# A two-layer graph kernel: the last item of layer two in four short sides and two batches, a later load of the path words, and saves by block

## The reference

```python
h = relu(layernorm(x))
# layer one: graph convolution with W, b; norm from the degrees
x = x + relu(segment_sum(norm[:, None] * (h @ W.T + b)[row], col))
h = relu(layernorm(x))
# layer two: rows of 16 segments x 32; 64 paths (i1, i2, i3) with coefficients
x1 = h[src].reshape(-1, 16, 32)
x2 = edge_attr_512.reshape(-1, 16, 32)
contrib = path_coeffs[None, :, None] * x1[:, i1, :] * x2[:, i2, :]
edge_out = zeros.at[:, i3, :].add(contrib)
out = zeros.at[dst].add(edge_out)          # x + out is returned
```

## Time and profile before

| | us |
|---|---|
| median of 3 runs (lowest, highest) | 1154.01 (1152.04, 1155.46) |
| the profiled execution's own time | 1154.45 |
| its span in the trace | 1152.8 |
| PE busy | 841.4 (73%) |
| DVE busy | 890.8 (77%) |
| ACT busy | 420.1 (36%) |
| POOL busy | 533.6 (46%) |
| mean granted TensorE clock | 0.849 of full speed |

### The profile page before, as it was taken

One profiled execution on the slowest core, in us unless ns is written; L12 is line 12 of the kernel. 1 busy time (PEld: TensorE's weight loads), 2 busy tenths in 40 slices (PEclk: granted clock), 3 DMA queues, 4 the chain that ended last, 5 costly groups with the idle time before them and its releaser, 6 DMA issues.

```text
span 1152.8 us, 21994 instructions
## 1 busy us (share of the span) xinstructions
PE 841.4 (73%) x5118; PEld 405.0 (35%) x5119; DVE 890.8 (77%) x1955; ACT 420.1 (36%) x1612; POOL 533.6 (46%) x610
## 2 busy tenths in 40 slices
PE   2788779990686967778696777859587785951985
PEld 1344333440341514324151432416142341510465
DVE  4667768440798989989898998989899898964600
ACT  4887886336024042332405133240513324013040
POOL 3222210435746555664656566465556656123010
PEclk9799998995887988989798898979988898985965
DMA  8000002135856556775655577575656767324000
GB/s 154 1 0 0 0 1 74 37 119 173 297 211 235 185 193 217 260 260 212 241 185 194 208 260 260 212 252 186 221 182 246 260 230 252 102 107 106 1 11 7
DMA packets 58553, 183.07 MB, mean 159 GB/s; under 512 B 19940, under 2 KB 20068, under 8 KB 52588
## 3 DMA queue, kind: packets, MB, share of 16 engines
q0 software_dynamic: 28528, 88.43, 24.4%
q1 hardware_dynamic: 21048, 88.36, 20.4%
q10 hardware_dynamic: 8900, 5.55, 1.8%
HBM read 173.45 MB, written 8.86 MB: 158 GB/s over the span
## 4 chain that ended last, share of the span: by engine, by line
DVE 31%; DVEq 25%; PE 20%; issue 15%; POOL 3%; ACT 2%; DMA 2%; SPq 1%; POOLq 0%; ACTq 0%
DVE q_mem L735 28%; DVEq L291 11%; DVEq L729 9%; PE psum L1067 5%; PE psum L1053 4%; PE psum L974 3%; PE psum L985 3%; PE psum L1008 2%; DVEq L735 2%; POOL x_mem L522 2%; DVE x_mem L656 1%; PE psum L999 1%; PE psum L971 1%; DMA x_mem<-in_L_gnn_W 1%; ACT hot_mem L823 1%
## 5 line engine op out<-in xcount | busy, mean ns | idle before, releaser
L735 DVE TENSOR_TENSOR q_mem<-x_mem 128x448 f32 (+1 forms) x1334 | 722.7, 622 | 104.6 <-DMA x_mem<-h_rows,src_now 55.6
L1067 PE MATMUL psum<-q_mem,hot_mem 128*32 128x512 f32 x2584 | 419.4, 719 | 206.5 <-DVE q_mem L735 193.9
L522 POOL DMA_INDIRECT x_mem<-h_rows,src_now x323 | 399.6, 1237 | 269.2 <-DVE q_mem L735 175.4
L1067 PEld LDWEIGHTS psum<-q_mem,hot_mem 128*32 128x32 f32 x2584 | 100.2, 127 | 485.5 <-issue 376.0
L1053 PEld LDWEIGHTS psum<-S,ident 128*128 128x128 f32 x1664 | 203.1, 203 | 33.3 <-issue 33.3
L1053 PE MATMUL psum<-S,ident 128*128 128x32 f32 x1664 | 208.6, 287 | 0.0
L908 ACT ACTIVATE S<-psum,coef 128x32 f32<-128x32 f32 (+1 forms) x832 | 153.1, 369 | 128.1 <-PE psum L1067 105.5
L914 ACT ACTIVATE acc<-psum 128x512 f32<-128x512 f32 x13 | 7.8, 597 | 456.7 <-PE psum L1053 391.3
L656 DVE TENSOR_SCALAR x_mem<-x_mem,spare 128x320 bf16<-128x320 f16 x324 | 79.1, 301 | 39.8 <-issue 39.8
L518 POOL DMA_DIRECT2D out<-acc x55 | 49.3, 896 | 105.7 <-ACT acc L914 82.6
L985 PE MATMUL psum<-x_mem,hot_mem 128*128 128x320 bf16 x324 | 68.4, 338 | 28.7 <-DVE x_mem L656 14.1
(11 more groups left out here) (156 smaller groups left out, 399.2 us busy)
## 6 DMA issues: line engine op xcount, KB each, us to landing
x_mem<-in_edge_attr SPq DMA_DIRECT2D x44, 1024.0 KB
x_mem<-in_edge_attr SPq DMA_DIRECT2D x44, 768.0 KB
x_mem<-h_rows,src_now POOLq DMA_INDIRECT x323
x_mem<-in_edge_attr SPq DMA_DIRECT2D x2, 1792.0 KB
out<-acc POOLq DMA_DIRECT2D x55, 64.0 KB
x_mem<-in_x SPq DMA_DIRECT2D x1, 2304.0 KB
out<-x_mem ACTq DMA_DIRECT2D x9, 256.0 KB
h_rows<-x_mem ACTq DMA_DIRECT2D x9, 256.0 KB, 2.0
```

Source lines behind the costliest of these rows:

```text
L522: pool.indirect_dma_start(x1[:, t, :], None, h2_dram[:, :], bass.IndirectOffsetOnAxis(ap=now[:, t - first:t - first + 1].bitcast(u32), axis=0)
L735: return nc.vector.tensor_tensor(q[s % 2][:, 0:tiles, p % PG, :], x1[:, first:first + tiles, ds(a, U)], x2[:, first:first + tiles, ds(b, U ...
L1067: last = nc.tensor.matmul(ps[g][side * M:(side + 1) * M, :], hot[:, first + k, :], q[s % 2][:, k, :, :].rearrange("p n u -> p (n u)"), sta ...
```

## The change

Five things, beside the renaming that follows from them.

1. **Last item.** FULL now counts full items (11). The 1826 edges of the last are four sides of 4, 4, 4 and 3 tiles (2 whole and one of 34 edges), cut in two batches of 8 and 7 tiles (`CUT_LAST`). POOL, DVE, ACT and PE run their ordinary two-batch code on it, SP a `load_last` with a wait for each batch. The final `save` takes each block after its own slot of the second batch. The last adds are four sides instead of three. COLS is 323. Indices are loaded by four DMAs for `dst` and four for `src` instead of two each; DVE's preparation has a few small reduces, copies and subtractions more.
2. **First turn.** The edge rows of three sides instead of two are loaded while layer one runs (`EARLY`), and the fourth waits for `agg_summed` alone. To make room, `counts_b`, `iota_i` and the pieces in `parts` are put elsewhere.
3. **Saves.** `save` gets the slots it waits for as a list. In the turns it is `[0, 1, G - 1, G - 1]`: blocks 2 and 3 both wait for slot 7 of the turn before, where block 2 waited for slot 6. In the final `save` it is each block's own slot.
4. **Blocks** are taken from `ORDER` and `ORDER_END`, both `[0, 1, 2, 3]`, which is the order of before.
5. **Path words.** DVE loads the next six words after the fourth product of six (`p % CHUNK == CHUNK // 2`), where it did after the first. This isn't in the change's title.

```diff
-    TL = 2 * T + 1
-    NORMAL, LAST_ITEM = [T, T, T, T], [T, T, 1, 1]
+    TL = 4
+    REST = E - FULL * P * TI
+    TR, TAIL = divmod(REST - (S4 - 1) * P * TL, P)
+    NORMAL, LAST_ITEM = [T] * S4, [TL] * (S4 - 1) + [TR + 1]
     CUT = [[(0, 4), (0, 4), (0, 3), (0, 3)], [(4, 7), (4, 7), (3, 7), (3, 7)]]
-    CUT_LAST = [(0, T), (0, T), (0, 1)]
+    CUT_LAST = [[(0, TL // 2)] * S4, [(TL // 2, n) for n in LAST_ITEM]]
+    ORDER, ORDER_END = [0, 1, 2, 3], [0, 1, 2, 3]
+    EARLY = 3
...
-            sp.dma_start(dst_i[:, 0:FULL * T].rearrange("p (b t) -> p b t", t=T), dst_full).then_inc(idx_in, 16)
-            sp.dma_start(dst_i[0:TAIL, FULL * T:FULL * T + 1], dst_tail).then_inc(idx_in, 16)
+            for to, edges in zip(by_column(dst_i), by_partition(dst)):
+                sp.dma_start(to, edges).then_inc(idx_in, 16)
...
                     for s in range(S4):
-                        if j == 0 and s == 2:
+                        if j == 0 and s == EARLY:
                             sp.wait_ge(agg_summed, C)
-                            for i in range(2):
-                                sp.wait_ge(h2_stored[i], 16 * (C // 2))
...
-            def load_last(turn):
-                sp.wait_ge(multiplied, group_before(turn, G - 1))
-                for s in range(2):
-                    if s:
-                        sp.wait_ge(multiplied, group_before(turn, TURN - 1))
-                    sp.dma_start(x2_mem[:, s * T * D:(s + 1) * T * D], edge_full[:, FULL - 2 + s, :]).then_inc(x2_last, 16)
-                sp.dma_start(x2[0:TAIL, 2 * T, :], edge_tail).then_inc(x2_last, 16)
+            def load_last(window, turn):
+                for j in range(2):
+                    at = tiles_before(CUT_LAST[j])
+                    sp.wait_ge(multiplied, group_before(turn, j * G + G - 1))
+                    if j:
+                        n = tiles_before(CUT_LAST[0])[-1]
+                        sp.wait_ge(x1_last[0], window * (16 * n) + 16 * n)
+                    for s in range(S4):
...
-            def gather_last(window, turn, at):
-                now = src_now[:, 0:TL]
-                for j in range(2):
-                    pool.wait_ge(multiplied, group_before(turn, j * G + G - 1))
...
-            for s in range(S4 - 1):
+            for s in range(S4):
                 add_rows(s, newer, total + 1)
...
                 for p in range(block * PG, min((block + 1) * PG, SURE)):
                     last = product(s, first, tiles, p)
-                    if p < STEADY and p % CHUNK == 0:
+                    if p < STEADY and p % CHUNK == CHUNK // 2:
                         load_pairs(p // CHUNK + 1)
-                last.then_inc(multiplied, done)
+                last.then_inc(multiplied, 1)
...
             def product_last(window, turn, at):
-                dve.wait_ge(x1_last, window * (16 * TL) + 16 * TL)
-                dve.wait_ge(x2_last, window * 48 + 48)
-                for g in range(G):
-                    product_slot(turn, g, 0, TL, 1 if g < G - 1 else 1 + G)
+                for j in range(2):
+                    n = tiles_before(CUT_LAST[j])[-1]
+                    dve.wait_ge(x1_last[j], window * (16 * n) + 16 * n)
+                    dve.wait_ge(x2_last[j], window * (16 * S4) + 16 * S4)
+                    for g, block in enumerate(ORDER if j == 0 else ORDER_END):
+                        product_slot(turn, j * G + g, block, j * TB, n)
...
-            def save(turn):
+            def save(turn, slots_done):
                 act.wait_ge(mixed, turn + 1)
-                for g in range(G):
-                    act.wait_ge(summed, group_before(turn, G + g))
-                    for p in range(g * PG, (g + 1) * PG):
+                for block in range(G):
+                    act.wait_ge(summed, group_before(turn, G + slots_done[block]))
+                    for p in range(block * PG, (block + 1) * PG):
...
                     if j == 0:
-                        save(turn)
+                        save(turn, [0, 1, G - 1, G - 1])
...
-            save(total)
+            save(total, ORDER_END)
```

More of the change, by code:

```diff
@@ L121, in gnn_layers_kernel @@
         in_agg, in_hot = Carve(x2_mem), Carve(hot_mem)
-        in_agg.take(2 * 4 * D)
+        in_agg.take(sum(b - a for a, b in CUT[0][0:EARLY]) * D)
         counts_b = in_agg.take(C * CW // 2).bitcast(bf16).rearrange("p (c n) -> p c n", c=C)
@@ L206, in gnn_layers_kernel @@
         acc = sb("acc", [P, D], fp32)
-        in_sums = Carve(S)
-        homes = ([in_hot.take(D // 2) for i in range(TI * M // (D // 2))]
-                 + [in_sums.take(D // 2) for i in range(NP * U // (D // 2))]
-                 + [in_iota.take(D // 2) for i in range(CW // (D // 2))])
-        homes += [in_agg.take(D // 2) for i in range(PARTS * C - len(homes))]
-        assert in_agg.at <= TI * D
+        more = sb("more", [P, 3 * (D // 2)], fp32)[:, :]
+        in_idx.at = 0
+        homes = []
+        for carve in (in_hot, Carve(S[:, :]), in_q, in_idx, Carve(bias_b), Carve(more), in_agg):
+            while carve.at + D // 2 <= carve.mem.shape[1] and len(homes) < PARTS * C:
+                homes.append(carve.take(D // 2))
+        assert len(homes) == PARTS * C
         parts = [[homes[i * C + c].bitcast(bf16) for c in range(C)] for i in range(PARTS)]
@@ L743, in late_products, with product_slot @@
                             product(s, first, tiles, m)
[L745 to L746 removed]
+            def product_slot(turn, s, block, first, tiles):
                 dve.wait_ge(summed, group(turn, s - 2))
                 dve.sem_inc(vector_steps, 1)
[L749 removed]
+                if block == G - 1:
                     late_products(s, first, tiles, SURE)
[L751 removed]
+                for p in range(block * PG, min((block + 1) * PG, SURE)):
                     last = product(s, first, tiles, p)
[L753 removed]
+                    if p < STEADY and p % CHUNK == CHUNK // 2:
                         load_pairs(p // CHUNK + 1)
[L755 removed]
+                last.then_inc(multiplied, 1)
             load_pairs(0)
@@ L1056, in mix, with sum_slot @@
                     last.then_inc(mixed, 1)
-            def sum_slot(turn, s, cut, first, begin, end, done):
-                g, at = s % G, tiles_before(cut)
+            def sum_slot(turn, s, block, cut):
+                j, at = s // G, tiles_before(cut)
                 pe.wait_ge(multiplied, group(turn, s))
@@ L1066, in sum_slot, with sum_turn @@
                             k = at[side] + t
-                            last = nc.tensor.matmul(ps[g][side * M:(side + 1) * M, :], hot[:, first + k, :],
+                            last = nc.tensor.matmul(ps[block][side * M:(side + 1) * M, :], hot[:, j * TB + k, :],
                                                     q[s % 2][:, k, :, :].rearrange("p n u -> p (n u)"),
-                                                    start=(begin and t == 0), stop=(end and t == b - a - 1))
-                last.then_inc(summed, done)
-            def sum_turn(window, turn, at):
+                                                    start=(j == 0 and t == 0), stop=(j == 1 and t == b - a - 1))
+                last.then_inc(summed, 1)
+            def sum_turn(turn, cuts, orders):
                 for j in range(2):
                     pe.wait_ge(hot_ready, turn * 2 + (j + 1))
-                    for g in range(G):
-                        sum_slot(turn, j * G + g, CUT[j], j * TB, j == 0, j == 1, 1)
+                    for g, block in enumerate(orders[j]):
+                        sum_slot(turn, j * G + g, block, cuts[j])
                         if j == 0:
```

182 lines of the change are left out of this document (88 added, 94 removed).

## The result

The changed kernel takes **1181.28 us** (median of 4 runs, 1174.66 to 1204.30), against 1153.83 (1152.04 to 1155.46, 4 runs) before: slower, by a ratio of 1.022 (95% interval 1.015 to 1.029; it leaves out the longest run, which stands over 1.5% above the shortest, and with all four the medians give 1.024). I had forecast 1128. The four times spread over 30 us, where those of before spread over 3. The profiled execution is the longest of the four (1204.30, span 1202.6); what it shows is one arrangement of a delay that comes and goes, so I use its rows for what happens, and the runs' times for how much.

A forecast was written before the change was run, and what follows sets the result against it. DVE's products were taken to bound the turns, PE close behind. Last product's end 1085.0, plus tail 48.0, minus steady 8, plus 1.5 gave a span of 1126.5; with 1.65 outside the span, 1128 us, range 1112 to 1144.

The forecast's parts named there:

- Start of each batch: DVE's batches in the turns: loading words behind the fourth product saves 0.88 us per first batch, 0.36 to 0.45 per second.
- The slower rival: Late saves throttle PE in every turn and its clock falls: 4.4 us in each of 10 turns, about 1180 us; chance 0.06.
- the sign: PE's granted clock in the turns changing by more than 0.03 from 0.849 would show the forecast wrong.
- Steady sum: All turns together: second batches -4.6 us, first batches -3.5 after PE and late saves, in sum -8; bounds -15 to +2.
- the later load buys nothing: Rival for the turns: lead is lost at long loads or PE sets slot 4; steady 0, 1136 us; chance 0.16.
- Last item: DVE's last-item products: hole gone, sequencer bounds batches of 24.9 and 30.3 us, last product ends at 1085.0 against 1089.8: -5.
- the rival of the lower clock in the last item: Item 10's four mixes on PE cost 6.9 us each instead of 3.76: 1138 us; chance 0.09.
- Tail: From the last product to the span's end: 48.0 us instead of 63.0, so -15, with final mixes of 27.3.
- The rival of full clock: Final mixes on PE run at full speed, 15.0 us instead of 27.3: 1116 us; chance 0.12.
- The rest: Preparation before layer two: more index DMAs and small DVE operations cost +1.5 us, bounds 0 and +3; other small terms about 0.

The follow-up runs named there:

- e1: Changed kernel with the six words loaded behind the first product of six again: 1135.21 us, ratio 0.984 to the kernel before.
- e2: Kernel before with only the later load added (behind the fourth product of six): 1209.84 us.
- g1: Changed kernel with the load behind the first product in the eleven full turns and behind the fourth in the last item alone: 1139.12 us, ratio 0.988.
- f2: e1 with blocks 2 and 3 saved after slots 6 and 7 as before: 1134.02 us.
- f1: Changed kernel with the later load only in first batches and the last item, behind the first product in the full turns' second batches: 1137.89 us.
- g4: Changed kernel with one of eight later loads moved three products earlier in each full turn's second batch: 1140.04 us, ratio 0.990.
- f4: e1 with wide matmuls that nothing reads on PE ahead of the last item's last two sums: 1133.92 us.
- g3: Changed kernel with the load late only in the last item and both adds of a batch behind its 14 gathers: 1139.24 us, ratio 0.989.

## Why the prediction was wrong

**The step that failed** is "Start of each batch". I followed the moved load through DVE's sequencer, DVE and PE, and priced each hole it closes as a gain. I never asked who used those holes, and so put what moving them does to POOL at nothing. A POOL read that has to wait beside DVE's two-operand products goes on at a break, and the breaks that I moved were the ones that let the gather behind the add go: it waited until product 25 and took 2.0 to 2.7 us before, and until product 48 and mostly 14.5 us after. Among my rivals none was about POOL, and my bounds for this term (-15 to +2) left the true value out by far: e1 against the changed kernel makes the later load 46 us dearer, e2 against before 56 (27 to 60 by its four runs). The trace of before had the signs: gathers of 0.95 us beside an idle DVE but about 1.30 beside a busy one, and the five that ended just behind a hole of DVE. What stays open is why a read at that place is held at all, when most go on: g1 shows one held with the early load too, so the later load makes the long holds common, and is not their only occasion.

**The slower rival had the number and the wrong cause.** It gave 1180 by late saves and a falling clock, 44 us. e1 keeps the late saves and takes 1135, and f2 shows no cost of them. The granted clock was 0.835 in the profiled execution (0.827 to 0.835 in the four) against 0.849, less than the 0.03 that I had named as the sign. That it comes with PE's longer waits is likely: in e1, where nothing in the turns waits for gathers, it was 0.843 to 0.856.

**Steady sum.** First batches did shrink as worked out, from 32.36 to 31.48 us in the mean (0.88 forecast). Second ones hardly did: 32.23 for 32.35, where I had 0.36 to 0.45, since four of them stood at 31.5 to 31.8 before already. And f1 shows that PE takes 6.7 of the 9.4 us gained on `issue` back. From the first product to the end of item 10 it is 733.6 us before, 733.4 in e1, 732.6 in f1 and 735.0 in g4. Even without long holds the term was near 0, not -8, as the rival "the later load buys nothing" had it (1136; e1 is 1135).

**Last item.** DVE's timeline after has these rows:

```profile
1096.57 1.47 DVE L750 TENSOR_TENSOR q_mem<-x_mem 128x256 f32 x4 [3.32 <-DMA x_mem<-h_rows,src_now]
...
1118.70 3.44 DVE L750 TENSOR_TENSOR q_mem<-x_mem 128x256 f32 x10 [0.40 <-issue]
1126.33 1.39 DVE L750 TENSOR_TENSOR q_mem<-x_mem 128x224 f32 x4 [4.18 <-PE psum L1077]
1129.09 2.04 DVE L750 TENSOR_TENSOR q_mem<-x_mem 128x224 f32 x6 [1.37 <-issue]
...
1153.12 3.37 DVE L750 TENSOR_TENSOR q_mem<-x_mem 128x224 f32 x10 [0.95 <-issue]
```

The first batch takes 25.6 us (24.9 forecast) and the second 30.2 (30.3): bound by the sequencer, with idle on `issue` between, and 0.34 us a product within a run. The hole of 23.8 is gone, but for 3.3 us behind a held gather. The wait for PE is 4.2 us instead of 1.7. The two mixes ahead of it, which I had at 3.76 us each, take 4.64 and 7.04 (timeline of PE):

```profile
1107.10 4.64 PE L1063 MATMUL psum<-S,ident 128*128 128x32 f32 x32
1111.67 3.64 PE L1077 MATMUL psum<-q_mem,hot_mem 128*32 128x512 f32 x16
1115.24 7.04 PE L1063 MATMUL psum<-S,ident 128*128 128x32 f32 x32
```

In e1 the wait is the same, and the four mixes take 4.20, 4.50, 7.04 and 7.04 us, so the rival of the lower clock in the last item came true in part. From the end of item 10 to the last product it is 63.2 us, and 61.3 to 64.5 in e1, f1, f2, f4 and g1 to g4, where I had 57.0 and the kernel before had 61.8. So this term brought nothing: what the hole gave back, the second round of unpacking and the slower mixes took.

**Tail.** The timelines of PE and POOL after:

```profile
1156.54 3.63 PE L1077 MATMUL psum<-q_mem,hot_mem 128*32 128x512 f32 x14 [0.69 <-DVE q_mem L750]
1160.64 24.40 PE L1063 MATMUL psum<-S,ident 128*128 128x32 f32 x128
...
1196.08 0.76 POOL L540 DMA_DIRECT2D out<-acc  x1 [2.54 <-DMA out<-acc]
```

From the last product (1156.49) to the span's end it is 46.1 us, forecast 48.0, before 63.0. The mixes took 24.4 instead of 27.3 us (27.52 before), since their first 3.4 us still ran at a granted clock of 0.95 in the mean; from 1165 on it was 0.50. My prediction had 0.50 for the whole chain behind the last product; the earlier trace rows shows it only from 1110.60. The rival of full clock (15.0) fell. The fourth add cost its 3.3 us.

**The rest.** The first product of layer two starts at 294.94, 0.6 us later than before, forecast 1.5, within its bounds.

**The sum without held reads.** Between the 22 batches of the turns DVE stands idle for 22 us in all before and for 97 after (added up over the batches' starts and ends). 1204.3 - 75 - 3.3 (ahead of the last item) gives 1126, by the forecast's 1128. But that agreement is luck: the long waits let PE catch up, so the batches that are left in this sum are 11 us shorter than before (700.8 us for 711.8), while in g4, with three short holds, they are 706.4 with more waits between, and the time is 1140. In e1 the turns take 0.2 us less than before, the last item 0.6 more, and the tail 44.2 us instead of 63.0. So e1's gain of 19 us is the tail's alone.

Best are e1, the changed kernel with its load put back, and its variants f2 and f4: 1134 to 1135 us, which these runs can't tell apart. f1, g1, g3 and g4 are at 1138 to 1140, beside other runs of the kernel before; none of them is shown to be faster than e1.

## What to carry to other kernels

Before an idle gap of one engine is closed, look at who else moves in it: here holes of 0.03 to 0.2 us on DVE, at the right place, were what let a held POOL read go, and moving them cost some 50 us. If an engine issues DMAs and shares an access with a busy one, look at the maximum of its instruction's time beside the median, and at what the long ones end behind. And a title's list isn't the diff: the one line that the title left out decided the case.

## What was not expected of the hardware

- DVE `tensor_tensor` with both inputs in SBUF, back to back at 0.536 us, held an indirect DMA of POOL for up to 25.8 us and a 14-element POOL copy for 29.6. A break in the stream of 0.03 us was enough to let a gather go; it ended 0.93 us later, and a held copy 0.05 to 0.06. With one input in PSUM nothing was held (maximum 1.19 us), and a gather took 0.95 us in the median instead of 1.28. POOL's DMAs without an index tile (at most 1.00 us) were not held in any run.
- Most reads in such a stream aren't held: they go on at one in three products (1.60 us). What makes one of them wait for a break isn't settled, nor why a few were let go without a visible one, at the end of a slot or behind a load of words.
- 128 mixes of 32 columns fell from a granted clock of 1.00 to 0.50 some 4 us behind their start, with PE busy throughout (e1, f4): 24.7 us, and 23.9 with wide matmuls placed ahead of them.
